# Reordering the head of a pipelined turn: where three stages' work stands on each engine

## Time and profile before

| | |
|---|---|
| Median of 3 runs | 1408.03 us (1408.01 to 1415.59) |
| Profiled execution | 1410.99 us, its span 1409.3 us |
| Mean granted clock of TensorE | 0.956 |
| TensorE busy | 1229.4 us, 87% |
| VectorE, ScalarE, GpSimd busy | 813.6, 607.0, 412.8 us |
| Chain that ended last | TensorE 72%, VectorE 11%, ScalarE 9%, issue 5% |
| Length of a full turn | 62.1 us |

### The profile page before, as it was taken

How to read it: one execution, slowest core, us unless ns; L and a number is a source line. 1 busy time by engine, 2 the same in 40 slices (tenths; PEclk the granted TensorE clock), 3 DMA queues, 4 the chain that set the end, 5 groups by cost and what they waited for, 6 DMA issues and landing times.

```text
span 1409.3 us, 29205 instructions
## 1 busy us (share of the span) xinstructions
PE 1229.4 (87%) x9542; PEld 920.3 (65%) x9543; DVE 813.6 (58%) x2110; ACT 607.0 (43%) x1288; POOL 412.8 (29%) x712
## 2 busy tenths in 40 slices
PE   5487699999999999999999999999987459999997
PEld 4265568777676878777677877778675335555554
DVE  4636377677677767767776766777654342122121
ACT  3435254554636355463636556363632112222221
POOL 2221113232231314223131412223132134544543
PEclk9598899999999999999999999999998769999999
DMA  8401620302022030202113020211255011211211
GB/s 270 105 0 46 268 87 23 117 27 92 30 89 87 33 119 15 104 30 89 63 56 119 15 104 30 89 58 69 106 190 214 30 30 56 60 56 55 63 56 35
DMA packets 51768, 112.29 MB, mean 80 GB/s; under 512 B 7333, under 2 KB 38863, under 8 KB 44944
## 3 DMA queue, kind: packets, MB, share of 16 engines
q1 hardware_dynamic: 45456, 96.81, 19.8%
q0 software_dynamic: 5616, 14.43, 3.5%
q10 hardware_dynamic: 656, 0.52, 0.1%
HBM read 89.72 MB, written 22.94 MB: 80 GB/s over the span
## 4 chain that ended last, share of the span: by engine, by line
PE 72%; DVE 11%; ACT 9%; issue 5%; DMA 2%; POOL 1%; ACTq 0%; DVEq 0%; SPq 0%; POOLq 0%
PE bank L1498 66%; PE bank L1533 2%; DVE a_p L1289 2%; ACT a_p L825 2%; PE bank L1700 2%; ACT shared L830 2%; DVE shared L1263 1%; PE bank L1862 1%; DVE a_sq L1257 1%; ACT shared L805 1%; ACT shared L877 1%; ACT b_qh L748 1%; DVE a_split L1226 1%; DVE a_split L1225 1%; ACT shared L810 0%
## 5 line engine op out<-in xcount | busy, mean ns | idle before, releaser
L1498 PE MATMUL bank<-shared 128*128 128x256 f32 (+4 forms) x1730 | 322.6, 376 | 36.7 <-POOL shared L1029 11.3
L1498 PEld LDWEIGHTS bank<-shared 128*128 128x128 f32 (+2 forms) x1730 | 220.8, 166 | 102.6 <-issue 29.9
L1289 DVE TENSOR_TENSOR a_p<-a_p,eb 128x385 f32<-128x385 f32 x256 | 125.9, 556 | 98.2 <-ACT a_p L825 98.2
L1498 PE MATMUL bank<-up,shared 128*128 x312 | 144.8, 608 | 11.0 <-issue 11.0
L990 POOL TENSOR_SCALAR a_rz<-a_ms 128x2 f32<-128x2 f32 x16 | 3.1, 193 | 425.8 <-ACT a_sq L839 425.8
L825 ACT ACTIVATE a_p<-bank 128x385 f32<-128x385 f32 x256 | 105.0, 501 | 42.1 <-PE bank L1498 42.0
L1475 DVE TENSOR_TENSOR shared<-bank,shared 128x512 f32<-128x512 f32 x39 | 27.0, 692 | 154.8 <-ACT shared L875 85.1
L1498 PEld LDWEIGHTS bank<-up,shared 128*128 128x128 f32 x312 | 57.2, 193 | 76.2 <-issue 76.2
L970 POOL TENSOR_TENSOR a_split<-a_sq,a_split 128x256 f16<-128x256 f32 x64 | 43.0, 702 | 162.9 <-ACT a_split L771 162.9
L875 ACT ACTIVATE shared<-bank 128x512 f32<-128x512 f32 x39 | 23.3, 597 | 138.1 <-PE bank L1498 132.6
L1498 PE MATMUL bank<-down,shared 128*128 x312 | 75.7, 385 | 7.2 <-ACT shared L877 7.2
(11 more groups left out here) (237 smaller groups left out, 2723.0 us busy)
## 6 DMA issues: line engine op xcount, KB each, us to landing
w_low<-low_w SPq DMA_DIRECT2D x44, 1024.0 KB, 4.8
up<-in_L_ffn_up_w SPq DMA_DIRECT2D x8, 1024.0 KB, 13.8
x_in<-in_x SPq DMA_DIRECT2D x16, 256.0 KB, 2.8
shared<-in_ctx SPq DMA_DIRECT2D x16, 256.0 KB, 2.8
rows_x<-shared SPq DMA_DIRECT2D x16, 256.0 KB, 2.2
rows_skip<-shared SPq DMA_DIRECT2D x16, 256.0 KB, 2.4
down<-in_L_ffn_down_w SPq DMA_DIRECT2D x8, 512.0 KB, 12.2
toep<-a_hT SPq DMA_DIRECT2D x1, 3072.0 KB, 10.2
```

The source lines that it names most:

```text
L1289: tt(a_p[:, n_ % NPA], a_p[:, n_ % NPA], eb[:, n_], ALU.mult).then_inc(sig["a_p"], 1)
L1498: return mm(out, lhsT=lhsT, rhs=rhs, start=first, stop=last, **kw)
```

## The change

The rows of the plan and the order in all engines' turns are changed; no operation is added or removed.

```
-PLAN = [a_s(0, 1), a_s(2, 3), ("lengths", "C", 0), ("out", "D", 0), ("out", "D", 1), ("rows", "C", 0)]
-PLAN += [b_s(0, 1, 2, 3), ("weigh", "A", 0), ("distances", "C", 0), ("out", "D", 2), ("expert", "C", 0)]
+PLAN = [a_s(0, 1), a_s(2, 3), ("scaled", "C", 0), ("out", "D", 0), ("out", "D", 1), ("rows", "C", 0)]
+PLAN += [b_s(0, 1, 2, 3), ("lengths", "C", 0), ("weigh", "A", 0), ("distances", "C", 0), ("out", "D", 2), ("expert", "C", 0)]
```

```
+            if Dd:
+                if it.first == SPLIT_FROM:
+                    pe.wait_ge(s_round["w11"], 16)
+                taken(pe, it, "D.q")
+                wait(pe, s_low_in["w11"], dd * 16 + 16)
+                split_cols_out(it, "D.h0", d_qT_hi, d_qT_low, w11_hi, w11_low, 0)
+            if Bb:
+                taken(pe, it, "B.x")
+                cols_out(it, "B.q_", b_xT, w1q, 0)
             if A:
...
                 rows_out(it, "A.v", a_xnT, w0v)
```

```
-            if Bb:
-                low("B.k", 1, b_kl, b_kh)
...
-            if A:
-                inverse_lengths(a, low_q)
+            def low_k():
                 if Bb:
-                    low("B.q_", 2, b_ql, b_qh)
+                    low("B.k", 1, b_kl, b_kh)
+            if A:
+                inverse_lengths(a, low_k)
```

```
+            if Bb:
+                if Dd:
+                    after(act, "x1_kept2", dd)
+                copy(x1_keep[:], x1[:]).then_inc(sig["x1_kept"], 1)
+            if Cc:
+                for t in range(T):
+                    nc.scalar.activation(c_x2[:, t], c_x2[:, t], ACT.Identity, scale=c_sc[:, 7, t:t + 1],
+                                         bias=c_sc[:, 9, t:t + 1]).then_inc(sig["c_rows"], 1)
+            if it.first == SPLIT_FROM - 1:
+                round_aside((2,))
             if A and it.first >= SPLIT_FROM:
```

```
                 after(sp, "b_p_used", it.batch("B"))
+                if it.first == SPLIT_FROM - 1:
+                    sp.wait_ge(s_low_out["w11"], 16)
                 sp.dma_start(flat(w11_low[:]).bitcast(F32), low_of["w11"].ap()).then_inc(s_low_in["w11"], 16)
+            if "C" in it.stages:
+                b = it.batch("C")
+                after(sp, "c_rows", b)
+                sp.dma_start(of_batch(x_rows, b), c_rows[:, :, 0:D]).then_inc(sig["c_stored"], 16)
+                sp.dma_start(of_batch(skip_rows, b), c_rows[:, :, D:]).then_inc(sig["c_stored"], 16)
```

More of the change, by code:

```diff
@@ L408, in flat @@
         return ap.rearrange("p a b -> p (a b)")
-    s_hi, s_low, s_round = (sem(n) for n in (
-        "weights_rounded_aside", "weights_low_parts_made", "weights_rounded"))
+    s_hi, s_low = (sem(n) for n in ("weights_rounded_aside", "weights_low_parts_made"))
+    s_round = {name: sem(f"rounded_{name}_in_place") for name in SPLIT}
     s_low_out, s_low_in = ({name: sem(f"low_part_of_{name}_{way}") for name in SPLIT} for way in ("out", "in"))
@@ L641, in turn @@
             if it.first == SPLIT_FROM:
+                for name in SPLIT:
+                    sp.wait_ge(s_low_out[name], 16)
                 full(sp, Turn(SPLIT_FROM - 1, 0), "A.out")
                 for name in SPLIT:
-                    sp.dma_start(flat(weight_hi[name][:]).bitcast(F32), hi_of[name].ap()).then_inc(s_round, 16)
+                    sp.dma_start(flat(weight_hi[name][:]).bitcast(F32), hi_of[name].ap()).then_inc(s_round[name], 16)
             if "P" in it.stages and it.first > 0:
@@ L659, in turn @@
                     sp.dma_start(low_of[name].ap(), made_low[n % 2].bitcast(F32)).then_inc(s_low_out[name], 16)
[L660 to L666, removed]
             if "A" in it.stages and it.first >= SPLIT_FROM:
@@ L728, in scaled_rows @@
                                          ).then_inc(sig["c_rows"], 1)
-            if it.first == SPLIT_FROM:
-                for name in SPLIT:
-                    act.wait_ge(s_low_out[name], 16)
             if A:
@@ L790, in turn @@
                 hidden(1)
-            if Cc:
-                scaled_rows()
             if Dd:
@@ L802, in turn @@
                 evacuate(it, "B.max", b_nmT[:].rearrange("p c s -> p (c s)"))
[L803 to L810, removed]
             for what, st, n in PLAN:
@@ L813, in turn @@
                     continue
+                if what == "scaled":
+                    scaled_rows()
                 if what == "lengths":
@@ L1236, in turn @@
                                       ALU.add).then_inc(sig["a_sumsq"], 1)
-            if Bb:
-                low("B.k", 1, b_kl, b_kh)
[L1240 to L1245, removed]
+            def low_k():
                 if Bb:
-                    low("B.q_", 2, b_ql, b_qh)
+                    low("B.k", 1, b_kl, b_kh)
             if A:
-                inverse_lengths(a, low_q)
+                inverse_lengths(a, low_k)
             else:
-                low_q()
+                low_k()
             if A:
@@ L1258, in turn @@
                        bc(a_rn[:, t], D0), ALU.mult).then_inc(e_sem(f"A.qk{t}"), 1)
+            if Bb:
+                low("B.q_", 2, b_ql, b_qh)
             def maxima(jobs):
@@ L1281, in turn @@
                                     ).then_inc(e_sem(f"A.q{t}"), 1)
+            if Cc:
+                after(dve, "c_norms", c)
+                for t in range(T):
+                    dve.scalar_tensor_tensor(c_rows[:, t, 0:D], c_x2[:, t], c_mv2[:, t, 0:1], vecs[:, FSC],
+                                             ALU.subtract, ALU.mult).then_inc(sig["c_xs"], 1)
+            if it.first == SPLIT_FROM - 1:
+                low_parts((0,))
             for what, st, n in PLAN:
@@ L1299, in turn @@
                 tt(a_xl[:], ps[:].rearrange("p (t n) -> p t n", n=D), a_xl[:], ALU.add).then_inc(e_sem("A.wo"), 1)
+            if it.first == SPLIT_FROM - 1:
+                low_parts((1,))
             if Bb:
@@ L1315, in turn @@
                 rest_of_hidden(it, (0, 1))
-            if it.first == SPLIT_FROM - 1:
-                low_parts((0,))
             if Bb:
@@ L1322, in turn @@
                 rest_of_hidden(it, (2,))
+            if it.first == SPLIT_FROM:
+                for name in SPLIT[::2]:
+                    dve.wait_ge(s_low_out[name], 16)
             if Dd:
@@ L1343, in turn @@
             if it.first == SPLIT_FROM - 1:
-                low_parts((1,))
+                low_parts((2,))
             if A:
@@ L1659, in turn @@
                     pe.wait_ge(s_top, 8)
[L1660 to L1668, removed]
             def rough(jobs):
@@ L1774, in turn @@
                 if it.first == SPLIT_FROM:
-                    pe.wait_ge(s_round, 16 * len(SPLIT))
+                    for name in ("w01", "w02"):
+                        pe.wait_ge(s_round[name], 16)
                 if it.first >= SPLIT_FROM:
```

13 lines of the change are left out of this document (6 added, 7 removed).

## The result

The changed kernel takes 1391.66 us (median of four runs, 1389.62 to 1393.71), the kernel before, run beside it, 1408.86 us: a ratio of 0.985, with a 95% interval of 0.981 to 0.990 (the two medians by themselves divide to 0.988). The profiled execution has a span of 1389.5 us against 1409.3, so 19.8 us are to be accounted for. The forecast was 1375 with a range of 1364 to 1389, so the median lies 2.7 us above the range. The start of turn 3 came as worked out; the thirteen turns gave 4.4 us instead of 15.6.

A forecast was written before the change was run, and what follows sets the result against it. TensorE bounds it, busy 58.69 of a full turn's 62.10 us. Gains 13.5 + 3.0 + 1.0 + 15.6 + 0.1 = 33.2 take 1410.99 to 1377.8; runs' median lies 3.0 lower: 1375 us, range 1364 to 1389.

The forecast's parts named there:

- Start of turn 3: Rounding made earlier in turn 2 frees 10.55 us of TensorE idling and 3.0 of slow-clock Q and K products: 13.5 us.
- the thirteen turns: Full turns and the one without P: 1.2 us gained in each, 15.6 in all; bounds nothing and 2.25 a turn.
- The rival that D.h0 waits: At turn 3, D.h0 waits for w11's rounded copy after all: 4 us less gain, 1379, inside the forecast's spread.
- Rest of turn 3: Turn 3 behind its start: maxima wait 1.4, B.q_'s low part 0.3, x1_keep 0.5, half of 1.7 for clock: 3.0 us.
- Head of a full turn: L1257's products start 3.3 us earlier, TensorE's following work starts no later, and B.m4 starts 2.0 us earlier.
- Middle of the turn: Part is given back: gaps of 1.0 us before C.xn's transposes and 1.1 before "weigh A 1", leaving 1.2 a turn.
- the turns give all back: Rival: lengths or scaled rows come another 1.2 us late, only 17.6 us are left, 1390 us; chance 0.18.
- The second gap stays away: Rival: VectorE gets through "expert" in time, a turn gains 2.25, 13.0 us more, 1362 us; chance 0.14.
- The clock in full turns: Rival: the clock falls in every turn because of the two new gaps, 1419 or 1437 us; chances 0.06 and 0.04.
- Turn 2 and tail: Turn 2 gains 1.0 us; turn 17 gains 0.9, turn 18 0.3, routing starts 1.1 later, tail together 0.1.

The follow-up runs named there:

- the experiment with this part alone: The kernel before with only the changes to turns 2 and 3, the order of the full turns as before; 1394.28 us, ratio 0.989.
- the last kernel: both_out2 plus turn 19's skip rows scaled early, C's distances ahead of the first A weighing, D's seventh output eighth ahead of the second B weighing; 1354.70 us, ratio 0.958.
- both_out2: The kernel with both edits, plus D's third output eighth ahead of the transposes of C's rows; 1362.40 us, ratio 0.964.
- the kernel with both edits: The changed kernel with ScalarE's lengths right behind its scaled rows and B.q_'s low part between VectorE's two normalised products; 1369.79 us, ratio 0.969.

## Why the prediction was right, and where it failed

**Start of turn 3.** Right in both parts: 10.55 of idle time foreseen, 10.7 measured, and 3.0 for the product's clock. No window of the turn's start is below a clock of 1.00, and the experiment with this part alone shows the same 13.7. That its medians lie 17.6 us apart, near the 16.5 forecast for the start and the rest of turn 3, is in part luck: 1.7 of its span's 16.8 came in the head of turn 17, where its clock was higher. D.h0 didn't wait for w11's rounded copy: the three copies landed 4.8, 6.9 and 8.9 us after their issue at 151.2 to 152.1, and D.h0 started at 157.85, so w11's was the first to land. The rival that D.h0 waits is out for the changed kernel. Where D.h0 waits for all three copies, it holds, with 3.54 us for the 4 foreseen.

**Rest of turn 3.** 3.3 us for 3.0, right as a sum and not by its terms. The wait for the maxima went (1.44). The one for b_ql, counted as a gain of 0.3, grew by 0.4 (0.29 to 0.69), and the one ahead of B's scores shrank by 0.5 (0.76 to 0.24). That leaves 1.8 for the clock, which the forecast had put at half of 1.7: no window up to 210 us is below 1.00.

**Head of a full turn: the step that failed.** I had the chain right (3.3 us earlier, 3.1 measured), then said that on TensorE "what follows starts no later" and took B.m4 as 2.0 earlier. It was 1.4. B.m2 takes bank 3, B.q_'s bank, and only the low part of B.q_ sets it free; the change put that behind both products of L1250. I counted its 0.6 against VectorE's maxima, and not against the bank of a matmul. TensorE waits 0.54 there, and B.v starts 13.2 us into the turn as before, not 0.5 sooner. Moving it between the products took the wait away and 0.57 from the turn.

**Middle of the turn.** The gap ahead of C.xn was 1.01 (1.0 foreseen), that ahead of "weigh A 1" 1.22 (1.1), both with the releasers named. But with the head 0.6 late, and 0.3 more (0.72 from C.xn's transposes to B's scores where I had 0.5, with exponentials and copies a tenth later here and there; not tested apart), the lengths ended 31.2 us into the turn instead of 30.3. What stands behind them moved with them, and the turn kept 0.3 of its 1.2. The weighing starts 34.99 us into the turn, against 35.21 before and 34.1 by the forecast. The rest of the turn gained 0.08, as forecast.

**The rivals.** That the turns give all back came nearest: it had 1390 and 17.6 us kept, measured were 1391.66 and 19.8. Its mechanism is the one found: the lengths come late. "The second gap stays away" would have been had for the move of one entry in the plan. The clock in full turns is 1.00 with three gaps in them. The Trainium skill's rule on swings of the gate between groups of matmuls (TensorE: Matmul & The Clock Gate, "A second HAM failure mode: psum-queue depth-cycling") had no hold on waits of 0.3 to 1.2 us here. In turn 17 it is less clear: in the last kernel the matmuls right behind a wait of 1.25 us ran at the lower clock (0.84 over 998 to 1008), in both_out2 those behind the same wait of 1.24 did not.

**Turn 2 and tail.** Turn 2 gained 1.2 (1.0). In turn 17 I gave 0.9 and it lost 1.2. Without stage A there is no A.v between the query product and the maxima, so TensorE waits 1.60 for b_ql, where three waits before made 1.15 (0.73, 0.19 and 0.23). So the gain didn't come. The loss is mostly the clock, 0.67 over the first 10 us against 0.83: at 0.83 the new order takes 13.87 us to B.v (both_out2) and the old 13.84.

```profile
1027.82 0.51 PE L1502 MATMUL bank<-b_kh,b_qh 32*128 32x256 f32 x8 [1.60 <-DVE b_ql L1199]
```

Turn 18 gained 1.2 (0.3), it too with a different clock (0.79 against 0.69 over its first 16 us). The routing starts 1.25 later after the scaled rows (1.1), and now waits for the stored rows:

```profile
1098.95 0.77 POOL L1020 IOTA shared<- 128x8 f32 x6 [8.20 <-DMA rows_skip<-shared]
```

## What to carry to other kernels

When work is moved behind something, list all that it releases: here a subtraction on one engine was also the release of a bank that a matmul two steps later claims. A gain at the head of a turn is worth what the last waits of the turn let through, so follow it to the end and look for an engine that idles just ahead of its late work: ScalarE had two gaps of 0.8 and 0.7 us there, and the lengths put in front of them gave nearly four times what the whole reordering of the turns had. Price the first and last turns by themselves, since cover that a full turn has may be missing in them. And when work goes ahead of other work, look at what its waits ask for: moved alone, D.h0 stood 3.54 us for copies that it doesn't read.

## What the runs showed of the hardware

The same early part of the program takes a different time from execution to execution. Turn 3's eight transposes started between 148.2 and 155.0 us in kernels whose order up to turn 2 is the same, and the granted clock goes with it; the changed kernel lies between (151.40, clock 0.90). Windows of 90 to 150 us, first of the kernel with both edits (turn 3 at 154.96), then of both_out2 (148.18):

```profile
90.00:150.00 60.00, 47.43 (x393) 33.32 (x394) 40.38 (x83) 30.62 (x55) 10.26 (x17) 0.87 0.25 99
```

```profile
90.00:150.00 60.00, 49.28 (x418) 36.22 (x417) 40.74 (x86) 32.09 (x58) 10.80 (x19) 0.94 0.36 135
```

The start of turn 17 shows the same: around one and the same wait of 3.65 us for d_qT_low, and with one order there, the mean clock of the first 10 us was 0.67, 0.83 or 1.00 in three kernels (the changed one, both_out2, the last), and the way to B.v took 14.99, 13.87 or 12.27 us. So the 4 us that the turned order of turn 17 seemed to cost are not shown to be the order's; what sets the clock there is open, with one profiled execution of each kernel. For terms of 1 to 4 us the length of the full turns, which agree within 0.1 us inside an execution, is the better measure than the median.
